# Two head groups in one output bank, a rearranged opening, another order of steps, and 26 fill matmuls

## The reference

```python
xn = _layernorm(x)
x = x + attn(xn, ...) + ffn(xn, ...)

# attn: 16 heads of 8, softmax within chunks of 16 tokens: once on neighbours, once on every third token
return _linear(local_out + atrous_out, Wo, bo)

# ffn: causal attention with 16 heads of 8 over 512 tokens (half of a head is rotated), then experts
x = x + mla(rmsnorm(x, w_ln1), ...)
x = x + moe(rmsnorm(x, w_ln2), ...)   # one shared expert and 7 routed ones (the best 2 per token, weighted)
```

## Time and profile before

| | |
|---|---|
| timed runs | 375.98 us, median of 3 (373.47 to 378.34) |
| the profiled execution | 371.83 us, its span 369.6 us |
| mean granted TensorE clock | 0.978 of 2.4 GHz |
| TensorE busy | 334.2 us, 90% of the span, 4504 matmuls |
| VectorE, ScalarE, GpSimd busy | 285.0, 222.3 and 123.0 us |
| chain that ended last | TensorE 60%, VectorE 28%, waits without a releaser 5%, ScalarE 3%, DMA 3% |

### The profile page before, as it was taken

How to read it: one execution, slowest core, us unless ns; L and a number is a source line. 1 busy time by engine, 2 the same in 40 slices (tenths; PEclk the granted TensorE clock), 3 DMA queues, 4 the chain that set the end, 5 groups by cost and what they waited for, 6 DMA issues and landing times.

```text
span 369.6 us, 11664 instructions
## 1 busy us (share of the span) xinstructions
PE 334.2 (90%) x4504; PEld 206.3 (56%) x4504; DVE 285.0 (77%) x720; ACT 222.3 (60%) x545; POOL 123.0 (33%) x148
## 2 busy tenths in 40 slices
PE   5779997898998989999989899888999999999994
PEld 5455664455564555565654565534546666656663
DVE  5979789799877988898998988987334577766743
ACT  5266345577675656677674766665765656456563
POOL 6186507040600826603312200000203563444443
PEclk9999999999999989999998999989999999999998
DMA  8435352222242123250222321106000000000000
GB/s 200 77 108 173 71 167 62 67 62 42 40 162 46 36 66 51 78 184 25 43 53 50 65 65 34 36 3 172 5 0 0 3 27 2 4 28 2 29 0 28
DMA packets 29141, 21.84 MB, mean 59 GB/s; under 512 B 12312, under 2 KB 26008, under 8 KB 29048
## 3 DMA queue, kind: packets, MB, share of 16 engines
q1 hardware_dynamic: 28872, 20.91, 22.8%
q10 hardware_dynamic: 216, 0.20, 0.2%
HBM read 6.81 MB, written 6.19 MB: 35 GB/s over the span
## 4 chain that ended last, share of the span: by engine, by line
PE 60%; DVE 28%; issue 5%; ACT 3%; DMA 3%; SPq 1%; POOL 0%; DVEq 0%; ACTq 0%; POOLq 0%
PE bank_B L1372 13%; DVE neg_max L1012 9%; PE bank_B L1180 8%; PE bank_c L1276 7%; PE bank_A L1378 7%; PE bank_A L1318 3%; PE bank_M L1283 2%; PE bank_B L1166 2%; DVE s_loc L1029 2%; DVE row_max L1026 2%; PE bank_M L1341 2%; PE bank_M L1221 2%; PE bank_c L1192 2%; PE bank_M L1211 1%; PE bank_M L1326 1%
## 5 line engine op out<-in xcount | busy, mean ns | idle before, releaser
L830 ACT ACTIVATE p_mla<-bank_B 128x512 f32<-128x512 f32 (+1 forms) x176 | 92.0, 561 | 54.6 <-PE bank_B L1166 31.0
L1012 DVE TENSOR_REDUCE neg_max<-bank_A 128x1 f32<-128x512 f32 (+3 forms) x176 | 106.9, 636 | 15.8 <-PE bank_A L1166 13.0
L1180 PE MATMUL bank_B<-q_stack,k_stack 54*128 54x512 bf16 (+3 forms) x256 | 62.4, 306 | 12.1 <-DVE neg_max L1012 8.2
L1159 PE MATMUL bank_A<-k_stack,q_stack 52*128 52x512 bf16 (+3 forms) x256 | 63.1, 307 | 3.2 <-DMA q_stack<-parts 2.2
L1372 PE MATMUL bank_B<-xrT,k_diag 128*128 128x512 f32 x128 | 60.9, 597 | 1.1 <-DVE k_diag L1137 1.1
L703 POOL TENSOR_TENSOR x<-x,q_part 128x512 f32<-128x512 f32 x31 | 39.5, 1274 | 58.0 <-ACT q_part L864 41.7
L1276 PE MATMUL bank_c<-p_mla,v_mla 128*32 128x384 f32 (+12 forms) x512 | 47.6, 453 | 0.4 <-ACT p_mla L830 0.4
L1180 PEld LDWEIGHTS bank_B<-q_stack,k_stack 54*128 54x128 bf16 x256 | 19.4, 94 | 49.6 <-issue 23.4
L864 ACT ACTIVATE q_part<-bank_A,expert_w 128x128 f32<-128x128 f32 x108 | 30.8, 369 | 24.6 <-PE bank_A L1378 24.6
L1137 DVE SCALAR_TENSOR_TENSOR k_diag<-k_diag,bank_B 128x512 f32<-128x512 f32 x32 | 22.0, 687 | 29.1 <-ACT k_diag L848 26.7
L1166 PE MATMUL bank_A<-masks 64*128 64x64 bf16 (+2 forms) x352 | 43.9, 204 | 0.0
(11 more groups left out here) (150 smaller groups left out, 550.4 us busy)
## 6 DMA issues: line engine op xcount, KB each, us to landing
v_dram<-v_rows SPq DMA_DIRECT2D x12, 324.0 KB, 3.8
k_stack<-parts SPq DMA_DIRECT2D x48, 64.0 KB
q_stack<-parts SPq DMA_DIRECT2D x45, 64.0 KB
k_diag<-k_part SPq DMA_DIRECT2D x48, 34.0 KB
v_diag<-v_dram SPq DMA_DIRECT2D x32, 45.0 KB, 2.1
v_diag<-v_dram SPq DMA_DIRECT2D x32, 36.0 KB, 1.9
v_dram<-v_rows SPq DMA_DIRECT2D x4, 283.5 KB, 2.8
x<-in_x SPq DMA_DIRECT2D x4, 256.0 KB, 7.8
```

What stands on the lines that cost most here:

```text
L830: drained_by(nc.scalar.activation(p_of(n)[:, m:m + len(heads), 0:w], src, ACT.Exp, scale=SCALE), step)
L1012: drained_by(nc.vector.tensor_reduce(neg_max[:, g, m:m + len(heads), i], src, AX.X, ALU.max, negate=True), step)
L1159: return nc.tensor.matmul(bank_of(step)[:, n * w:(n + 1) * w], q_stack[b % 2][rows, h % 8, i * P:(i + 1) * P], k_stack[b % 2][rows, h % 8, ...
L1180: nc.tensor.matmul(bank_of(step)[:, m * w:(m + 1) * w], k_stack[b % 2][rows, h % 8, j * P:(j + 1) * P], q_stack[b % 2][rows, h % 8, j * P: ...
```

## The change

1. **Two head groups share one round of `bank_c`.** The values `v_mla` are laid out with zeros between the heads, 18 columns per head, so that the 32 columns that a matmul issues put one group's 9 results in the first half of a strip's 18 rows and add zeros to the other's. Groups 0 and 1, and 2 and 3, add into the same bank; the copy to `oT_mla` and the step `Y` come once per two groups, 8 times instead of 16, and `Y` on VectorE works on twice the size. To match, the heads are dealt to the groups in another order (the copies into `w_mla`).
2. **The opening.** The first transpose, `MA.0.1`, `LK.0`, `LQ.0` and `MV.0` use the banks B instead of M (`EARLY_IN_B`). Two small tails of kT and qT move from VectorE to ScalarE, two memsets (one of them now of all of `v_mla`) from VectorE to GpSimd, half of the copies that make `k_part` of batch 0 from GpSimd to ScalarE, and one rounding of k on ScalarE from behind `XT.0.0` to behind those copies.
3. **The order of all steps** is another.
4. **Dummies.** `WARM` has 26 instead of 30, at other steps. `FILL` adds 26 matmuls of 192 columns in bf16 at seven E steps, 2 to 5 at each, into the bank that the step (or, with no S step beside it, the next DOWN step) is about to write. For that TensorE's wait for the E step's bank stands first and that for the S step's bank behind the fills; before, the S step's stood first.

```diff
-WARM = {("WF",): 6, ("XT", 0, 1): 2, ("MA", 0, 0): 2, ("S", 0, 0): 10, **{("S", 0, n): 1 for n in range(2, 12)}}
+WARM = {("LQ", 0): 5, ("LV", 0, 1): 7, ("S", 0, 0): 10, ("XT", 0, 0): 1, ("XT", 0, 1): 3}
+FILLS = {
+    2: """
+    E.3.1.0.1
+    """,
+    3: """
+    E.2.3.0.0 E.3.0.0.0
+    """,
+    4: """
+    E.1.3.0.0 E.2.2.1.1
+    """,
+    5: """
+    E.1.1.0.1 E.2.1.1.2
+    """,
+}
+FILL_WIDTH = 192
...
+EARLY_IN_B = {("XT", 0, 0), ("MA", 0, 1), ("LK", 0), ("LQ", 0), ("MV", 0)}
...
 ORDER = """
-LN.0 WF XT.0.1 MA.0.0 MB.0 MA.0.1 XT.0.0 ST.0.0 LK.0 LQ.0 STATS.1 ST2.0 MV.0 ROOT LV.0.0 KD.0.0 * KD.0.1 * KD.0.2
-LV.0.1 *3 KD.0.3 LN.1 *2 LV.0.2 XT.1.0 STATS.2 VD.0.0 LS.0.0 * LK.1 LR.0.0 LQ.1 *2 PT.0.0 * LS.0.1 * SHIFT.0.0
...
+LN.0 WF XT.0.1 MA.0.0 MB.0 MV.0 STATS.1 XT.0.0 MA.0.1 LK.0 LQ.0 LV.0.0 LV.0.1 ROOT ST.0.0 LV.0.2 STATS.2 KD.0.0
+KD.0.1 KD.0.2 KD.0.3 LN.1 VD.0.0 *2 XT.1.0 * ST2.0 *4 LS.0.0 LK.1 LR.0.0 *2 LQ.1 * PT.0.0 * LS.0.1 LO.0.0 LR.0.1 *2
...
-        v_mla = sb("v_mla", [P, 2, NT, H, HD + 1])
+        v_mla = sb("v_mla", [P, 2, NT, H + 1, 2 * (HD + 1)])
...
+            nc.gpsimd.memset(s_loc[:], 0.0).then_inc(ones_set, 1)
+            nc.gpsimd.memset(v_mla[:], 0.0).then_inc(v_mla_zeroed, 1)
+            pool.wait_ge(v_mla_zeroed, 1)
+            nc.gpsimd.memset(v_mla[:, :, :, 0:H, 2 * HD + 1:], 1.0).then_inc(ones_set, 1)
...
+                    if b == 0:
+                        wait_drained(act, step)
+                        act.wait_ge(v_rows_set, 1)
+                        for par in range(2):
+                            for dst, src in k_halves(1, par):
+                                ins = nc.scalar.copy(dst, src)
+                        ins.then_inc(k_part_by_act, 1)
+                        act.wait_ge(rest_ready, 1)
+                        nc.scalar.copy(parts[:, 0, 1, :], rest[:]).then_inc(rounded[0], 1)
...
-                elif kind == "PV" and step[3] == NT - 1:
+                elif kind == "PV" and step[3] == NT - 1 and step[2] % 2:
...
-                        y_mla[:, :, 4 * HD * g:4 * HD * g + 4 * HD].rearrange("p i (h d) -> p i h d", h=4), o[:, :, :, 0:HD],
-                        den.unsqueeze(3).broadcast_to((P, NT, 4, HD)), ALU.mult), step)
+                        y_places[:, :, c:c + 2 * HD].rearrange("p n (a d) -> p n a d", a=2), o[:, :, :, 0:HD],
+                        den.unsqueeze(3).broadcast_to((P, H, 2, HD)), ALU.mult), step)
...
+            def fill(step, to):
+
+                for _ in range(FILL.get(step, 0)):
+                    nc.tensor.matmul(to[:, 0:FILL_WIDTH], masks[:, 0:P], masks[:, 0:FILL_WIDTH], start=True,
+                                     stop=True, skip_group_check=True)
...
+                    if other:
+                        wait_free(pe, step)
+                        fill(step, bank)
+                        wait_free(pe, other)
+                    else:
+                        if step in FILL:
+                            wait_free(pe, next_down[step])
+                            fill(step, bank_of(next_down[step]))
+                        wait_free(pe, step)
...
-                    if j == 0 and n > 1:
-                        pe.wait_ge(c_drained, (n - 1) // NT)
+                    second = g % 2
+                    if j == 0 and not second and n > 1:
+                        pe.wait_ge(c_drained, (n - 1) // (2 * NT))
...
-                        first = (HD + 1) * (4 * g + m)
-                        width = min(PV_WIDTH, H * (HD + 1) - first)
+                        first = (HD + 1) * (2 * (4 * m + g) + 1 - second)
+                        width = min(PV_WIDTH, 2 * (HD + 1) * (H + 1) - first)
```

More of the change, by code:

```diff
@@ L217, in bank_uses @@
         return [("A", step)]
-    if kind == "E":
+    if kind == "E" or step in EARLY_IN_B:
         return [("B", step)]
@@ L292, in build @@
     waits_for_e = set(beside.values())
+    next_down, ahead = {}, None
+    for step in reversed(steps):
+        ahead = step if step[0] == "DOWN" else ahead
+        next_down[step] = ahead
     with ExitStack() as ctx:
@@ L742, in _ @@
                     drain(step, dst, bank[:], scale=cols[:, 3:4] if step[2] else None)
-                    if step == ("XT", 0, 0):
-                        act.wait_ge(rest_ready, 1)
-                        nc.scalar.copy(parts[:, 0, 1, :], rest[:]).then_inc(rounded[0], 1)
                 elif kind == "LQ":
@@ L1192, in _ @@
                     nc.tensor.matmul(bank_c[:, 0:P], eye[:], eye[:], start=True, stop=True)
-                if step in where and kind != "SHIFT":
-                    wait_free(pe, step)
+                if step in where:
                     bank = bank_of(step)
+                    if kind not in ("S", "E", "SHIFT"):
+                        wait_free(pe, step)
                 if kind == "WF":
@@ L1237, in _ @@
                     if step not in waits_for_e:
+                        fill(step, bank_c)
+                        wait_free(pe, step)
                         for n in range(len(UNITS[step[2]][1])):
```

142 lines of the change are left out of this document (78 added, 64 removed).

## The result

The changed kernel takes 376.5 us (median of 20 runs, 372.5 to 380.67). The kernel before takes 373.4 us in the 20 runs taken beside it (369.76 to 385.05). The ratio is 1.0086 with a 95% interval of 1.006 to 1.0113: **slower by 0.9%**, some 3.2 us, where 365.1 us and a gain were forecast. By 2% the two are the same, but the interval leaves out 1, and 376.5 us lies outside the range. Every ratio here compares, of each kernel, the runs within 1.5% of its fastest (19 and 14 of these 20); the means of all 20 runs stand 0.4% apart.

The account below looks back on a forecast made before the run. TensorE was taken to bound the experts and, in turns with VectorE, the attention. Terms -5.0 - 0.5 - 2.5 - 3.4 + 0.5 = -10.9 from the profiled 371.83 us gave 360.9, plus 4.15 a median of 365.1 us; range 357 to 376.

Parts of the forecast that it names:

- Two head groups in one bank: Attention: eight of sixteen Y steps go, 5.6 us leave TensorE; 5.0 us counted off the path, ends 0 and 5.6.
- VectorE's -0.5: Attention: VectorE's Y work, paired, takes 2.5 us less; 0.5 us counted as gain, ends 0 and 2.5.
- The rival in which VectorE binds: Attention: TensorE's saving buys idle time, Y term 0, VectorE's 2.5; sum -7.9, 368.1 us; chance 0.12.
- my 91%: Attention, 40 to 262 us: TensorE busy 202.81 of 222 us, the share used to take 5.0 us off the path.
- The order of the rest: Steps otherwise the same in another order: TensorE's idle 19.2 us can shrink or grow; 0, ends 5 either way.
- The tightest place of the shift rows themselves is looser: SP's queue: the shift rows' tightest place has more room in the new order, while batch 1's last stack load has less.
- The prediction's own sign for it: Sign of a wrong forecast for SP's order: idle TensorE ahead of score matmuls with a DMA of the stacks as releaser.
- The opening: Before the attention: first local row_max at 33.6 instead of 36.66 us; 2.5 us gain, ends 4.5 gain and 3 loss.
- The rival with the low clock: Opening stays at the low level, ten passes some 0.35 us longer each; term from -2.5 to +3, 370.6 us; chance 0.08.
- The clock: Attention: four falls cost 6.7 us, 1.7 us each; with the fills half is counted as gained, 3.4 us.
- The fills: Attention: 26 matmuls of 192 columns cost TensorE 0.5 us on the path, ends 0 and 2.1.
- The slower rival: Attention's pairs of scores and maxima: clock falls more often, deciding from nine falls on, 376.9 us; chance 0.08.

Follow-up runs that it names:

- two pairs: Rebuilt opening against before's opening, both without fills: 1.006 against 1.0005, and with SHIFT.2.3 ahead of ST.3.5 and VD.3.0, 0.9976 against 0.9933.
- the word moved: SHIFT.2.3 put ahead of ST.3.5 and VD.3.0 in the order; done to the changed kernel it gave 1.0027 of before, against 1.0086.
- the mended opening: Changed kernel, POOL's clearing held back, k's second rounding earlier, batch 1's statistics, transposes, normalization and POOL's two roots later: 1.0012 of before.
- y_rest_shift: Kernel before's opening and dummies, the pairing, the changed kernel's order behind the opening, no fills, SHIFT.2.3 ahead of ST.3.5 and VD.3.0: 0.9933 of before.
- y_rest: Kernel before's opening and dummies with the pairing, and the changed kernel's order from the first local scores on, no fills: 1.0005 of before.
- a_nofill: The changed kernel without its 26 fills: 1.006 of before.
- The pairing alone: Kernel before with two head groups per output bank, eight Y steps; order, opening and dummies as before: 0.9916 of before, 3.1 us less.

## Why the prediction was wrong

Taken one after the other, the runs give the terms: the pairing -3.1 us (0.9916); the new order behind the opening +3.3 (1.0005); the rebuilt opening +2.1 (1.006, or 1.8 from two pairs); the fills +1.0 (1.0086). The sum is +3.2 us, the measured loss, as it must be; each term but the first is known to 2 or 2.5 us only. Against the sum of the prediction:

- **Two head groups in one bank, -5.0 and VectorE's -0.5.** The gain is there, -3.1, and its size was off. The step that failed is "at TensorE's 91% share I take 5.0 us off the path". 5.8 us of transposes did go; 3.4 us came back as waits ahead of the exponentials. The rival in which VectorE binds, with -2.5, lies within the interval of 1.7 to 4.6; the forecast's 5.5 doesn't. The Trainium skill (Perfetto Trace Analysis, Identifying the Most-Contended Engine), which does not take matmul busy time as TensorE's measure, was nearer here than my 91%: the longer waits of TensorE were for VectorE's maxima, 8.2 us before and 10.2 with the pairing.
- **The order of the rest, 0 with ends of 5.** This is the step that turned the sign. "The tightest place of the shift rows themselves is looser" was false for SHIFT.2.3: the order puts it behind ST.3.5 and VD.3.0 on SP, and I counted score steps between the shift and its use, but not the issue time of the eleven loads ahead of it on the queue, 3.05 + 3.71 us by the rows above. (The sixteen of k_diag stay ahead of it with the word moved, and the wait is gone.) The prediction's own sign for it, idle TensorE with a DMA of the stacks as releaser, appeared at 218.9 us, ahead of an exponential's matmuls.
- **The opening, -2.5.** Measured +1.8 (0.1 to 3.5), with what else differs in those pairs. The step that failed is "k_part is ready at about 24 us as before, since its other half now waits for a rounding that ScalarE does after its own copies": this names the wait and counts it at nothing. k_part was ready at 27.28, and behind it stood twelve k_diag products of ScalarE (7.78 us) that the sum did not have; two roots of POOL ahead of q_part, which it did not have either, made q_part end at 35.46. So the first local row_max came at 37.60 instead of 33.6. The rival with the low clock had its place and its size about right, but not the whole of its reason: four passes of the projections, not ten, ran at the low level, and the clock then fell once more at about 33 us. How much of the 1.8 us is the chain's stays open: the mended opening shortens it and gains, but before's opening, in the one profiled execution of y_rest_shift, had its first local row_max at 39.05 us.
- **The clock, -3.4.** In the runs that the ratio compares, the change spends 2 x (1 - 0.9751) x 375.7 = 18.7 us at the low level as the profile counts it, the kernel before 16.7 (at 0.9777). So the clock gave nothing. The step that failed is "the order is another, so the stretches are too; I take half": the mean clock is 0.9790 with the new order behind before's opening (y_rest), 0.9721 with the rebuilt opening too (a_nofill), and the fills bring only 0.9751 back. The price of a fall was too high besides. Over all 114 runs of the kernel before, time rises by 0.35 us for each microsecond at the low level (correlation 0.91), so a fall of 3.4 us goes with 1.2 us, where the sum had 1.7. Probably part of the low time lies beside waits that would be there anyway; no run shows it.
- **The fills, +0.5.** 1.0 to 1.9 us, near the upper end of 2.1, and each known to 2 us.

The slower rival, at 376.9 us, came close to the measured time by accident: it needed at least nine falls, some 31 us at the low level, and the runs have 18.7. That the order itself could cost had only been in the bounds, with no mechanism, and with a sum of -10.9 in front of it these bounds reached 376.0 at most. The time the prediction started from was another small error: the three runs shown have a median of 375.98 us, the 114 later ones 374.0. Two slips in it change nothing: VectorE's 1.72 us in the earlier trace rows are of 3 us, not of 4, and twenty-six fills of 0.085 us are 2.2 us, not 2.1.

## What to carry to other kernels

When an order of steps is rewritten, price each queue at its tight places by issue time: add up the lengths of all the issues that now stand between a transfer's data and its own issue, not the number of steps. A unit of work taken off the engine that seems to bind is worth what is left after the next engine's waits; do it alone first, for here one part of four was the only one that gained. Dummy matmuls that raise the granted clock are no gain by that: look at the time, since each of them stands in the queue ahead of work, and took 0.79 us there instead of 0.49 where the clock was low. And one profiled execution is not the kernel: the place of the falls, and 4.4 us at the end of the opening, differed between two that ran the same program.

## What the runs showed of the hardware

- With each microsecond more at the lower clock level (1.2 GHz) the time of the kernel before is 0.35 us longer (114 runs), that of the other kernels 0.27 to 0.49 (6 to 20 runs each). This is a relation between runs, not an experiment. The Trainium skill (TensorE: Matmul & The Clock Gate, Terms) puts the penalty at the throttled time times the share of the pulses that is missing, which is 0.5; none of these slopes reaches it.
- The same instructions can keep the clock or lose it. The pairing alone and y_rest_shift have the same instructions on TensorE until 27 us and nearly the same times from 16 us on, with a wait of 1.87 and 1.89 us before the first score matmul; in the one the clock reads 1.00 from there to 47 us (the row below; y_rest_shift's is the third of its kind above), in the other it falls at about 27 us and the mean of 27 to 47 is 0.66. They were not alike ahead of it: y_rest_shift's clock had read 0.53 from 10 to 12 us. In the profiled executions of the openings of before's kind it fell in three of five, in the change's in all six that have it as it is or with the clearing held back or ten dummies more.

```profile
27.00:47.00 20.00, 18.64 (x291) 12.64 (x292) 17.79 (x42) 11.59 (x24) 12.65 (x20) 1.00 0.41 118
```

- VectorE's tensor_scalar from SBUF to SBUF took 2.28 us beside a POOL memset and 1.11 apart from it. The Trainium skill (SBUF — State Buffer, Who interferes with whom) says that a tensor_scalar can enter a mode with two ports, in which it and an instruction of GpSimd hold a shared pair of ports in turn. The two numbers agree with that; which mode the instruction ran in no run shows.
- On SP's queue sixteen k_diag loads of one step take 11.73 us to issue, 0.73 us each, three stack loads 3.05 and eight of v_diag 3.71; what stands behind them waits for that.
